# A graph network kernel: the nodes outside of the pairs as blocks of 128 and 20 instead of 74 and 74 in H1 and in the third layer, the short block's high and low parts in one stationary tile

## The reference, cut to what matters

```
h = relu(layernorm(x))                 # x: 2708 x 512
h = relu(adj @ (h @ W1) + b1)          # adj: 2708 x 2708, W1: 512 x 1024
h = relu(adj @ (h @ W2) + b2)          # W2: 1024 x 1024
out = x + adj @ (h @ W3) + b3          # W3: 1024 x 512
```

## Time and profile before

| | |
|---|---|
| Time, median of 3 runs | 1578.43 us (1577.51 to 1580.37) |
| The profiled execution: time | 1577.23 us |
| The profiled execution: span, first to last instruction | 1575.4 us |
| TensorE (PE) busy | 1569.8 us, 100% of the span, 7638 matmuls |
| DVE busy | 878.7 us, 56% |
| ACT busy | 643.5 us, 41% |
| POOL busy | 530.6 us, 34% |
| Granted TensorE clock | 1.00 in every slice |
| DMA moved | 334.52 MB, mean 212 GB/s |

### The profile page before, as it was taken

How to read it: one execution, slowest core, us unless ns; L and a number is a source line. 1 busy time by engine, 2 the same in 40 slices (tenths; PEclk the granted TensorE clock), 3 DMA queues, 4 the chain that set the end, 5 groups by cost and what they waited for, 6 DMA issues and landing times.

```text
span 1575.4 us, 21103 instructions
## 1 busy us (share of the span) xinstructions
PE 1569.8 (100%) x7638; PEld 1352.6 (86%) x7638; DVE 878.7 (56%) x1360; ACT 643.5 (41%) x1145; POOL 530.6 (34%) x488
## 2 busy tenths in 40 slices
PE   9999999999999999999999999999999999999999
PEld 7888889988889898989898989888898888888898
DVE  8983433255453546353545444764665537676766
ACT  5542222233343424233333333543455436555554
POOL 5864554436655545000000003573202333021302
PEclk9999999999999999999999999999999999999999
DMA  6966657555687888454657567783544357898887
GB/s 242 347 192 225 221 181 223 177 161 157 194 273 239 296 265 292 144 178 116 204 150 220 171 209 237 256 274 111 182 130 124 95 167 239 255 326 263 264 271 223
DMA packets 211091, 334.52 MB, mean 212 GB/s; under 512 B 25608, under 2 KB 96896, under 8 KB 210988
## 3 DMA queue, kind: packets, MB, share of 16 engines
q1 hardware_dynamic: 171484, 239.78, 49.6%
q0 software_dynamic: 15680, 55.31, 10.7%
q10 hardware_dynamic: 23824, 38.10, 6.8%
HBM read 243.75 MB, written 89.36 MB: 211 GB/s over the span
## 4 chain that ended last, share of the span: by engine, by line
PE 98%; DVE 1%; DMA 1%; ACT 0%; issue 0%; DVEq 0%; ACTq 0%
PE ps L1820 32%; PE ps L1822 31%; PE ps L1821 31%; PE ps L1910 2%; PE ps L1909 2%; DMA raw<-HX 0%; PE ps L1858 0%; DVE ring L1451 0%; DMA xin<-x 0%; DVE slots L1433 0%; ACT slots L1164 0%; DVE stats L1363 0%; DVE parts L1580 0%; DVE still L1399 0%; DVE parts L1576 0%
## 5 line engine op out<-in xcount | busy, mean ns | idle before, releaser
L1451 DVE TENSOR_TENSOR ring<-raw,ring 128x512 fp32r<-128x512 f32 (+1 forms) x522 | 381.4, 745 | 398.0 <-ACT ring L1202 395.8
L1202 ACT CAST ring<-raw 128x512 fp32r<-128x512 f32 (+1 forms) x564 | 320.2, 576 | 487.4 <-PE ps L1822 392.6
L1820 PE MATMUL ps<-slots,still 128*128 128x512 f32 (+1 forms) x504 | 183.2, 364 | 0.7 <-DVE slots L1433 0.5
L1821 PE MATMUL ps<-slots,still 128*128 128x512 f32 (+1 forms) x504 | 183.1, 363 | 0.0
L1822 PE MATMUL ps<-slots,still 128*128 128x512 f32 (+1 forms) x504 | 183.1, 363 | 0.0
L1820 PE MATMUL ps<-ring,even 128*128 128x512 f32 (+1 forms) x480 | 174.3, 363 | 0.0
L1821 PE MATMUL ps<-ring,even 128*128 128x512 f32 (+1 forms) x480 | 174.3, 363 | 0.0
L1822 PE MATMUL ps<-ring,even 128*128 128x512 f32 (+1 forms) x480 | 174.3, 363 | 0.0
L1820 PE MATMUL ps<-ring,S 128*128 128x512 f32 (+1 forms) x420 | 153.4, 365 | 0.3 <-DVE ring L1451 0.2
L1821 PE MATMUL ps<-ring,S 128*128 128x512 f32 (+1 forms) x420 | 152.8, 364 | 0.0
L1822 PE MATMUL ps<-ring,S 128*128 128x512 f32 (+1 forms) x420 | 152.8, 364 | 0.0
(11 more groups left out here) (160 smaller groups left out, 3022.1 us busy)
## 6 DMA issues: line engine op xcount, KB each, us to landing
raw<-TS SPq DMA_DIRECT2D x160, 256.0 KB, 3.3
raw<-adjT SPq DMA_DIRECT2D x122, 256.0 KB, 3.8
raw<-adjT SPq DMA_DIRECT2D x41, 512.0 KB, 5.0
TS<-made SPq DMA_DIRECT2D x20, 1024.0 KB, 6.7
raw<-TS SPq DMA_DIRECT2D x80, 165.0 KB, 2.8
raw<-HS SPq DMA_DIRECT2D x50, 256.0 KB, 3.2
raw<-P SPq DMA_DIRECT2D x44, 256.0 KB, 4.0
HS<-pair_buf POOLq DMA_DIRECT2D x20, 512.0 KB, 4.7
```

The costliest lines, as they stand in the source:

```text
L1202: act.copy(hi, src).then_inc(hi_done, 1)
L1451: dve.tensor_tensor(lo, src, hi.bitcast(F32), ALU.subtract).then_inc(lo_done, 1)
L1820: pe.matmul(out, st_hi, mv_hi, start=start, stop=False)
L1821: pe.matmul(out, st_hi, mv_lo, start=False, stop=False)
```

## The change

**Blocks.** Block 20 is now 128 nodes and block 21 (`SHORT`) 20 nodes (`TAIL`). The pairing for the sums stays 74 by 74: stack k (k = 0, 1) is 64 nodes of block 20 and 10 nodes of block 21. The host lays out `adjX` in that order.

**Short block.** In the stationary tile of block 21 the 20 nodes are loaded twice, in columns 0 to 19 and 32 to 51 of each slice. ACT casts the whole tile; DVE replaces columns 32 to 63 by the low part. Two matmuls then take the place of three: (high, low) by the moving high part, and by the moving low part. Rows 0 to 31 and 32 to 63 of PSUM are added afterwards on DVE: in H1 with a copy, the b1 addition and an addition for each half, in w3 with a copy and an addition, after which ACT copies the sum to the buffer.

**Stores.** Block 20's results are spread over both stacks by `store_full`, 12 DMAs (of 64, 32, 22, 64, 22 and 22 rows for each k), block 21's by `store_short`, 6 DMAs of 10 rows. This holds in H1 and in w3. In H1 block 20 now stores all 1024 columns. In w3 there is a step "keep" after each of the two blocks, where there was one after block 21.

**Sums.** POOL loads both stacks back from HX (or HX3) with two DMAs and waits for them before it forms EXTRA's sums.

```diff
+TAIL = 2 * REST - P
+KEPT = 18
 def first_node(block):
-    return block * P if block <= 2 * PAIRS else 2 * PAIRS * P + REST
+    return block * P
 def block_runs(block):
     first = first_node(block)
-    return [(0, first, P)] if block < 2 * PAIRS else [(0, first, REST), (REST, first, AGAIN)]
+    return [(0, first, P)] if block < SHORT else [(0, first, TAIL), (STEP, first, TAIL)]
...
-                if b == 21:
-                    p.steps.append(("keep", (bufs, p.copied)))
+                if pair_of(b) == EXTRA:
+                    p.steps.append(("keep", (b, buf, p.copied)))
+                if b == 20:
+                    return
+                if b == SHORT:
                     p.comb += 4
...
+        def store_full(engine, where, tile, stored):
+            for k in range(2):
+                rows = tile[k * MOST:(k + 1) * MOST]
+                first, second = where(k, 0), where(k, 1)
+                engine.dma_start(first[0:MOST], rows).then_inc(stored, 16)
+                engine.dma_start(first[REST:REST + STEP], rows[0:STEP]).then_inc(stored, 16)
+                engine.dma_start(first[REST + STEP:P], rows[STEP:AGAIN]).then_inc(stored, 16)
+                engine.dma_start(second[0:MOST], rows).then_inc(stored, 16)
+                for row in (MOST, LOW):
+                    engine.dma_start(second[row:row + MOST + STEP - REST], rows[REST - STEP:MOST]).then_inc(stored, 16)
+        def store_short(engine, where, tile, stored):
+            for k in range(2):
+                rows = tile[k * TAIL // 2:(k + 1) * TAIL // 2]
+                engine.dma_start(where(k, 0)[MOST:REST], rows).then_inc(stored, 16)
+                for row in (LOW, P):
+                    engine.dma_start(where(k, 1)[row + MOST - REST:row], rows).then_inc(stored, 16)
...
                     if g.block == 20:
                         act.wait_ge(relu_done, n)
-                        store_stacked(act, HX[EXTRA_PLACE[X11], 0], HX[EXTRA_PLACE[X11], 1], tile[:, 0:F], stored)
-                    elif g.block == 21:
+                        store_full(act, kept1, tile.rearrange("p (s f) -> p s f", s=2), stored)
+                    elif g.block == SHORT:
                         act.wait_ge(relu_done, n)
...
+                        store_short(act, kept1, tile.rearrange("p (s f) -> p s f", s=2), stored)
...
+                    if g.block == SHORT:
+                        act.wait_ge(joined, 6)
+                        act.copy(buffer(buf)[0:STEP], spill_1[0:STEP, :]).then_inc(copied, 1)
+                        continue
...
+                    (store_short if b == SHORT else store_full)(act, kept3, tile, kept3_stored)
...
+                        if g.block == SHORT:
+                            out = pair_buf[0:STEP, i, side, cols]
+                            if half:
+                                dve.wait_ge(drained, number - 1)
+                            dve.tensor_copy(spill_1[0:STEP, :], ps[STEP:2 * STEP, g.banks[half], :]).then_inc(joined, 1)
+                            dve.tensor_tensor(out, ps[0:STEP, g.banks[half], :], b1_rows[0:STEP, cols], ALU.add) \
+                                .then_inc(joined, 1)
+                            dve.wait_ge(joined, 2 * half + 2)
+                            dve.tensor_tensor(out, out, spill_1[0:STEP, :], ALU.add).then_inc(drained, 1)
+                            continue
...
+                if pair == EXTRA:
+                    for k, tile in enumerate((A, B)):
+                        pool.dma_start(tile.rearrange("p (s f) -> p s f", s=2), kept1(k, 0)).then_inc(extra_in, 16)
+                    pool.wait_ge(extra_in, 32)
...
+                            if g.block == SHORT:
+                                pe.matmul(ps[:, g.banks[half], :], hi, mv[0], start=start, stop=False)
+                                mm = pe.matmul(ps[:, g.banks[half], :], hi, mv[1], start=False, stop=stop)
+                            else:
+                                mm = three(ps[:, g.banks[half], :], hi, lo, mv[0], mv[1], start=start, stop=stop)
```

More of the change, by code:

```diff
@@ L1064, in load @@
                 elif j.kind == "extra3":
-                    which, value = (kept3_stored, 128) if j.part in (X11, X12, X22) else (sums3_stored, 128)
+                    which, value = (kept3_stored, 16 * KEPT) if j.part in (X11, X12, X22) else (sums3_stored, 128)
                     if which not in waited:
@@ L1446, in cut @@
                 hi, lo, src = cut_tile(j)
-                if j.kind == "extra2":
+                if j.block == SHORT:
+                    hi, src = (a.rearrange("p (k i) -> p k i", k=KF)[:, :, STEP:2 * STEP] for a in (hi, src))
+                    lo = hi
+                elif j.kind == "extra2":
                     hi, lo, src = (a[0:REST, :] for a in (hi, lo, src))
@@ L1492, in _ @@
                         dve.wait_ge(group_done, g.done[half])
+                        if g.block == SHORT:
[8 more added lines that the diff above has]
+                            continue
                         dve.tensor_tensor(pair_buf[:, i, side, cols], ps[:, g.banks[half], :], b1_rows[:, cols],
                                           ALU.add).then_inc(drained, 1)
+                elif kind == "block":
+                    g = a[0]
+                    if g.block == SHORT:
+                        low = spill_1[0:STEP, :]
+                        dve.wait_ge(g_stored[1], plan.stored["g", 1])
+                        dve.wait_ge(group_done, g.done[0])
+                        dve.tensor_copy(low, ps[STEP:2 * STEP, g.banks[0], :]).then_inc(joined, 1)
+                        dve.wait_ge(joined, 5)
+                        dve.tensor_tensor(low, ps[0:STEP, g.banks[0], :], low, ALU.add).then_inc(joined, 1)
                 elif kind == "stat":
@@ L1629, in combine1 @@
                 if pair == EXTRA:
-                    store_stacked(pool, *(HX[3:5, k].rearrange("s p f -> p s f") for k in range(2)),
+                    store_stacked(pool, *(HX[4:6, k].rearrange("s p f -> p s f") for k in range(2)),
                                   A.rearrange("p (s f) -> p s f", s=2), sums_stored[i])
@@ L1636, in combine1 @@
                 if pair == EXTRA:
-                    store_stacked(pool, *(HX[5:7, k].rearrange("s p f -> p s f") for k in range(2)),
+                    store_stacked(pool, *(HX[6:8, k].rearrange("s p f -> p s f") for k in range(2)),
                                   B.rearrange("p (s f) -> p s f", s=2), sums_stored[i])
@@ L1646, in combine3 @@
                 if pair == EXTRA:
-                    pool.wait_ge(kept3_stored, 128)
+                    pool.wait_ge(kept3_stored, 16 * KEPT)
+                    for k, tile in enumerate((A, B)):
+                        pool.dma_start(tile.rearrange("p (s f) -> p s f", s=2), kept3(k, 0)).then_inc(extra_in, 16)
+                    pool.wait_ge(extra_in, 64)
                 else:
@@ L1893, in block_group @@
                                 mv = [W3c[:, n * KF + q, i, :] for i in range(2)]
-                            mm = three(ps[:, g.banks[half], :], hi, lo, mv[0], mv[1], start=n == 0 and q == 0,
-                                       stop=n == len(g.tiles) - 1 and q == KF - 1)
+                            start, stop = n == 0 and q == 0, n == len(g.tiles) - 1 and q == KF - 1
+                            if g.block == SHORT:
+                                pe.matmul(ps[:, g.banks[half], :], hi, mv[0], start=start, stop=False)
+                                mm = pe.matmul(ps[:, g.banks[half], :], hi, mv[1], start=False, stop=stop)
+                            else:
+                                mm = three(ps[:, g.banks[half], :], hi, lo, mv[0], mv[1], start=start, stop=stop)
                         if g.phase == "h1" and half == 0:
@@ L2000 @@
         "x": x, "xT": halves(x.T), "adjT": adjT,
-        "adjX": np.stack([stacks(adjT[rest:rest + REST]), stacks(adjT[rest + REST:])]), "W1": W1, "W2": W2, "W3": W3, "b1": b1,
+        "adjX": np.stack([stacks(np.concatenate([adjT[rest + k * MOST:rest + (k + 1) * MOST],
+                                          adjT[rest + P + k * TAIL // 2:rest + P + (k + 1) * TAIL // 2]]))
+                          for k in range(2)]), "W1": W1, "W2": W2, "W3": W3, "b1": b1,
         "b2T": b2.reshape(-1, P).T, "b3T": b3.reshape(-1, P).T,
```

30 lines of the change are left out of this document (15 added, 15 removed).

## The result

The changed kernel takes 1590.83 us (median of 4 runs, 1589.99 to 1593.69), the kernel before 1577.97 us beside it (4 runs, 1576.97 to 1580.37). The ratio is 1.0078, 95% interval 1.0066 to 1.0090: slower, as forecast, by 12.9 us between the medians (10.4 to 14.2 by the interval). The profiled execution is the slowest of the four, 1593.69 us with a span of 1591.5 us.

What follows compares the result with a forecast made beforehand. TensorE was taken as the bound, busy for the whole span without slack. To the profiled 1577.2 us, H1 added 6.8 and w3 6.9, giving 1590.9; with 1.2 for the median, 1592.1 us (0.87% slower), range 1583 to 1601.

Steps and rivals of the forecast that it cites:

- four places named: TensorE idle before groups 19 and 20 of H1 and inside groups 18 and 19 of w3, some 17 us in all.
- one sign that the prediction had named as wrong: In the profile after, DMA issues of 10 and 22 rows no longer than those of 32 would count against the prediction.
- Matmuls removed, -3.6 us: Block 21 takes 16 matmuls in place of 24 in H1 and w3: 3.63 us less, 1.81 us in each stage.
- `store_full`, 8.1 us in both stages: Block 20's 12 issues on ACT: six at 0.53 us, six at 0.82 us; bounds 6.4 and 10.0 us.
- `store_short`, 4.9 us: Block 21's six issues on ACT at 0.82 us each; bounds 3.2 and 6.8 us.
- few rows, 0.82 us: Issues of 10 and 22 rows on ACT priced at 0.82 us each, from SP's loads of 20 rows.
- H1, tile 19: TensorE waits 2.5 us for this tile's low part, its cast standing behind `store_full` on ACT; bounds 0.7 and 4.4 us.
- H1, tile 20: TensorE waits 6.1 us behind block 21's DVE additions, ACT's relu and six issues; bounds 4.4 and 8.0 us.
- w3, group 18: TensorE waits 5.2 us for the group's second tile, its cast behind block 20's 12 issues; bounds 3.5 and 7.1 us.
- w3, group 19: TensorE waits 3.5 us for the group's second tile, behind block 21's additions, copy and six issues; bounds 1.8 and 5.4 us.
- rival 5: TensorE's clock falls to 1.2 GHz after the two longest waits, costing 5.4 us: 1595 to 1598 us; chance 0.16.
- POOL and the loads, nothing: POOL waits longer and loads 1 MB (0.5 MB in w3), but its sums are wanted late enough: no time counted.

Runs made afterwards that it cites:

- e1: Changed kernel with the short block's third matmul added back (16 matmuls more): 1592.48 us, ratio 1.0077 to the kernel before.
- e3: Changed kernel with half the columns of block 20's H1 stores issued by POOL, the other half by ACT: 1593.69 us, ratio 1.0085.
- e4: Changed kernel with the H1 steps of blocks 20 and 21 moved behind the cut of tile 20, issues still on ACT: 1585.71 us, ratio 1.0038.
- e6: Changed kernel with POOL's two HS stores (1 MB) of the pair before EXTRA issued after EXTRA's stores landed: 1590.85 us, ratio 1.0074.
- e10: Changed kernel with POOL issuing the 18 stores in H1 only, ACT still issuing them in w3: 1581.30 us, ratio 1.0010.
- e5: Changed kernel with all 18 stores of blocks 20 and 21 on POOL in H1 and w3, none on ACT: 1576.93 us, ratio 0.9989.

## Why the prediction was right, and where its terms were off

The mechanism is the forecast one: four waits at the four places named, each behind ACT's issues. That the time came out so close (1592.1 forecast, 1590.83 measured) is luck: H1 was forecast at +6.8 us and w3 at +6.9, and by the measured terms they are +9.9 and +1.7. Single terms were wrong by up to 4 us in both directions, and one sign that the prediction had named as wrong came true: issues of 10 and 22 rows are no longer than those of 32.

- **Matmuls removed, -3.6 us.** The count is right. The gain shows only where the casts are in time (2.7 us with POOL's stores); in the changed kernel the waits swallow it (e1).
- **`store_full`, 8.1 us in both stages: mis-sized.** 11.9 us in H1, 6.7 us in w3. In H1 the prediction saw 0.97 us an issue in the earlier trace rows and set it aside with "so bytes don't decide above that". That row of the kernel before stood under full DMA engines too, as this window on ACT of the kernel before shows (same columns):

```profile
417.50:421.50 4.00, 0.11 (x1) 1.00 1.03 392
```

  The row was to be read with the DMA share of its moment. Its 12 x 0.97 = 11.6 us would have been nearly right, as the mean of unequal halves: 0.75 us an issue in the first six, 1.24 in the second, which fell beside POOL's 1 MB.
- **`store_short`, 4.9 us: mis-sized.** 2.2 us in both stages. 10-row issues are 0.28 to 0.36 us each. The class "few rows, 0.82 us", taken from SP's loads, doesn't carry over to them: it set a load on SP beside the first store of a row of stores on ACT. The Trainium skill says in "DMA: Bandwidth & Descriptors", section "Why a DMA increments its semaphore by 16 and not by 1", that the issuing sequencer writes the increments of the engines that a DMA doesn't use. The trace shows no cost of it that could be told: in w3 10-row stores (0.28 to 0.36 us) and 22-row stores (0.37 to 0.57 us) are shorter than those of 32 and 64 rows (0.60 to 0.62 us).
- **H1, tile 19.** 2.5 us forecast, 6.3 measured; the 3.8 us between are `store_full`'s.
- **H1, tile 20.** 6.1 forecast, 2.0 measured: 2.7 less for `store_short`; 0.25 more for DVE's chain (427.67 to 431.99, 4.3 us for 4.05 forecast); and 1.7 less because group 19 ran at the low clock and so wanted the tile later, while the chain on DVE and ACT kept its pace.
- **w3, group 18.** 5.2 forecast, 2.7 measured: 1.4 less for the issues, and 1.1 less because they began at 1287.11, beside the stationary casts of the pair. The prediction had them behind these casts, by the one in-order queue that the kernel's description gives ACT.
- **w3, group 19.** 3.5 forecast, 0.8 measured, 2.7 less for `store_short`.
- **The clock, rival 5, 0.16.** It came true in H1, after the 6.3 us wait and once more after the 2.0 us one; here the trace agrees with what the Trainium skill says in "TensorE: Matmul & The Clock Gate", section "HAM oscillation — how this bites in real kernels", that pauses bring the clock down. In this execution the clock stayed at 1.00 after w3's waits. It cost 1.7 us twice, but the first 1.7 came off the next wait, and the time stayed under rival 5's 1595 to 1598 us.
- **POOL and the loads, nothing.** Right: no wait at the start of pass 2 or of pass 3.

With measured terms H1 is -1.8 + 6.3 + 1.7 + 2.0 + 1.7 = +9.9 us and w3 -1.8 + 2.7 + 0.8 = +1.7, in sum +11.6 us, inside the measured 10.4 to 14.2. The 1.3 us to the difference of the medians are not assigned. The profiled execution is 16.5 us over that of before. Beside the 11.6 us it has 2.9 us of idle time before pass 1's matmuls, where before had 0.7 and which the change doesn't touch, 0.7 us in the W2 stage (before: none) and 0.9 us in pass 3 (before: 0.2 us of such a wait in all).

## What to carry to other kernels

DMA issues are work of the engine that issues them: count those that an edit puts ahead of something wanted on an in-order queue, and read the price of one from a row with the same DMA share before one with the same number of rows. This is a first guess only: at a share of 0.90 an issue took 0.8 us here, at 0.88 in e3 another took 2.5. When TensorE is the bound, move them to an engine whose next reader is far off before counting on removed matmuls; here that turned 1.0078 into 0.9989. Where forecast errors can cancel, test the stages apart.

## What the runs showed of the hardware that was not expected

- An issue of a 10-row store on ACT took 0.28 to 0.36 us with the DMA share at 0.32 to 0.36, and up to 2.55 us for the same store with it at 0.93 to 1.02. Postponing 1 MB of another queue's stores took six issues from 7.4 to 4.6 us; moving half of ACT's bytes to POOL at the same moment didn't shorten its issues. What in the queue holds the issue, these profiles don't show.
- ACT went on to issue DMAs before casts that stand earlier in its program had begun (an issue at 1287.11, such casts from 1287.29 and 1287.90). The other way round, casts behind issues did wait for them.
- TensorE's clock fell to its lower level within a wait of 6.3 us and was back after 3.3 us of matmuls, fell again 1.0 us after a wait of 2.0 us, and stayed up after waits of 2.7 and 0.8 us. The length of a wait alone doesn't tell which it will be: at the same place in w3 it stayed up after 2.5 us in e4 and fell after 2.5 us in e6 and 2.8 us in e10, and in the W2 stage it fell after 2.3 us in e5.
